# Attention pass A masked through the 32 empty contraction rows, pass B one and a half quads behind it

## The reference

```python
x = x + 0.5 * ffn(layernorm(x))                  # int4 weights with LoRA
x = x + attention(layernorm(x))                  # the one that is changed
x = x + 0.5 * ffn(layernorm(x))
x = x + 0.5 * moe(layernorm(x))
x = x + linear_attention(layernorm(x))
x = x + 0.5 * moe(layernorm(x))

def attention(x, W_attn, W_proj):                # 16 heads of 16
    q, k, v = split(x @ W_attn.T)
    sets = [(i*L, (i+1)*L - 1) for L in (4, 8, 16, ..., 1024) for i in range(T // L)]
    K, V = sums of k, v over each set            # 511 sets
    logits = where(t >= last token of the set, q @ K.T * scale, -inf)
    tail   = sum(q * K_tail) * scale             # the open block of four tokens
    att = softmax(concat(logits, tail))
    out = att[..., :-1] @ V + att[..., -1:] * V_tail
    return out @ W_proj.T
```

## Time and profile before

| | us |
|---|---|
| median of 3 runs | 1737.92 (1735.68 to 1743.44) |
| profiled execution | 1737.69 |
| its span, first to last instruction | 1736.0 |
| TensorE busy | 1433.7 (83%) |
| VectorE busy | 988.1 (57%) |
| ScalarE busy | 689.3 (40%) |
| GpSimd busy | 561.6 (32%) |

### The profile page before, as it was taken

The page is one execution under the profiler, slowest core; times in us unless marked ns, Lnnn a source line. Parts: engine busy times, 40 slices in busy tenths (PEclk is TensorE's granted clock), DMA queues, the critical chain, the costliest instruction groups (busy, mean ns, idle before and its releaser), DMA issues. The chain is left out here.

```text
span 1736.0 us, 26631 instructions
## 1 busy us (share of the span) xinstructions
PE 1433.7 (83%) x9328; PEld 1075.2 (62%) x9328; DVE 988.1 (57%) x2872; ACT 689.3 (40%) x1640; POOL 561.6 (32%) x465
## 2 busy tenths in 40 slices
PE   6899899999999678439999998388994379899894
PEld 5566544555554455228888887365662369788793
DVE  8887777787873597875531111366675945421120
ACT  4222157666667376325423222013334445222221
POOL 6522300000000342304536564322212143447634
PEclk9989989999999898559999999699996579999997
DMA  3034552333300032315869894510114146779963
GB/s 107 19 130 134 136 117 57 81 57 81 57 26 2 1 109 85 149 29 159 250 173 318 241 254 95 137 37 25 49 62 173 22 111 221 201 232 237 278 188 42
DMA packets 113475, 211.82 MB, mean 122 GB/s; under 512 B 20069, under 2 KB 79370, under 8 KB 104138
## 3 DMA queue, kind: packets, MB, share of 16 engines
q1 hardware_dynamic: 87338, 178.93, 32.2%
q0 software_dynamic: 26016, 31.34, 11.6%
HBM read 158.71 MB, written 51.12 MB: 121 GB/s over the span
## 5 line engine op out<-in xcount | busy, mean ns | idle before, releaser
L952 DVE TENSOR_REDUCE attnm_top<-psum 128x1 f32<-128x384 f32 (+3 forms) x384 | 212.7, 596 | 56.5 <-PE psum L1037 52.3
L1174 ACT ACTIVATE attnm_prob<-psum 128x512 f32<-128x512 f32 (+1 forms) x384 | 192.1, 530 | 86.3 <-PE psum L1047 79.7
L2545 DVE SCALAR_TENSOR_TENSOR moe2e_h<-moe2e_gate,psum 128x160 f32<-128x160 f32 x160 | 50.3, 320 | 206.4 <-ACT moe2e_gate L2481 164.3
L2413 PE MATMUL psum<-moe2e_xgT,moe_w_up 128*128 128x160 f32 x1024 | 154.3, 309 | 11.5 <-ACT moe2e_xgT L2490 6.0
L2545 DVE SCALAR_TENSOR_TENSOR moe1e_h<-moe1e_gate,psum 128x160 f32<-128x160 f32 x160 | 50.1, 320 | 193.5 <-ACT moe1e_gate L2481 152.1
L2413 PEld LDWEIGHTS psum<-moe2e_xgT,moe_w_up 128*128 128x128 f32 x1024 | 148.5, 197 | 14.8 <-issue 13.9
L2344 POOL DMA_INDIRECT out<-moe2e_y,moe_scatter_i x74 | 116.5, 1574 | 118.8 <-DMA out<-moe2e_y,moe_scatter_i 54.5
L2344 POOL DMA_INDIRECT x_sum<-moe1e_y,moe_scatter_i x74 | 116.8, 1579 | 116.2 <-DMA x_sum<-moe1e_y,moe_scatter_i 57.3
L2413 PE MATMUL psum<-moe1e_xgT,moe_w_up 128*128 128x160 f32 x1024 | 149.5, 302 | 4.6 <-ACT moe1e_xgT L2490 2.8
L2413 PEld LDWEIGHTS psum<-moe1e_xgT,moe_w_up 128*128 128x128 f32 x1024 | 143.5, 192 | 8.2 <-issue 7.2
L1348 POOL DMA_INDIRECT moe_xg<-xn_rows,moe_gather_i x80 | 83.8, 1048 | 164.6 <-DVE moe_gather_i L1537 93.0
(11 more groups left out here) (420 smaller groups left out, 3110.5 us busy)
## 6 DMA issues: line engine op xcount, KB each, us to landing
moe_w_up<-in_expert_up SPq DMA_DIRECT2D x64, 1024.0 KB
moe_w_down<-in_expert_down SPq DMA_DIRECT2D x64, 512.0 KB
attnm_q_hat<-q_parts SPq DMA_DIRECT2D x72, 128.0 KB, 4.4
moe_a_up<-in_adapter_up SPq DMA_DIRECT2D x32, 256.0 KB
q_parts<-attnf_q_part SPq DMA_DIRECT2D x12, 512.0 KB, 2.8
attnm_k_hat<-k_parts SPq DMA_DIRECT2D x72, 64.0 KB, 2.3
x_res<-in_x SPq DMA_DIRECT2D x8, 512.0 KB
v_tails<-attnf_v_tail SPq DMA_DIRECT2D x4, 1024.0 KB, 5.3
```

The source lines that it names most:

```text
L952: nc.vector.tensor_reduce(top[:, n // QUADS % 2, tiles[0]:tiles[-1] + 1, hh:hh + 1], s.ps[:, u.bank, 0:len(tiles) * width].rearrange("p (t ...
L1174: nc.scalar.activation(prob[:, i % NPROB, at:GROUP], s.ps[:, u.bank, at:GROUP], ACT.Exp).then_inc(taken[u.bank], 1)
L2413: ins = nc.tensor.matmul(s.ps[:, u.bank, half * CAP:(half + 1) * CAP], lhsT, xgT[:, q, c, k * CAP:(k + 1) * CAP], start=(c == 0), stop=(c ...
L2545: nc.vector.scalar_tensor_tensor(out=h[:, HELD[n], i, :], in0=gate[:, i, :], scalar=1.0 if i < INTER // P else SCALE_A, in1=s.ps[:, u.bank ...
```

## The change

1. The sets are laid out in blocks of 64 instead of 128, so that the sets ending within token tile i are block i. `larger` and the mask's maker follow; the mask in `mask_f` takes six selects over both halves, one memset and one select. mask_ts and its copy on VectorE go.
2. Pass A has no mask products. The mask is a product of its own rows: rows 96 to 127 of q_hat and k_hat, until now empty, hold a token's and a set's part. A tile takes one product of the 96 rows over the sets of earlier tiles and one of all 128 rows over its own 64. The columns of a head fall from 3584 to 2300; VectorE takes one reduction per tile, eight per head instead of six, over 2300 instead of 2560 columns.
3. These rows are made by GpSimd in the front stage, once, behind the tails of batch 0 (`make_rows`): two memsets, six selects, a memset, two selects, and two copies that repeat them over k_first (2048 elements per partition) and q_first (4096). SP writes them to HBM; `load_rows` brings them with each quad, 32 rows for quads 1 to 4 (128 and 256 KB), the three that B overwrites for the later ones.
4. B overwrites row 96 to 98 of k_hat with ones and of q_hat with the maxima, so GpSimd writes the ones after each pass A of a quad, before B: sixteen memsets of 3 x 2048 in its order with the tail multiplications.
5. B runs LAG = 38 slots behind A instead of 48; the output steps keep their distance to B; MT stands before slot 5 instead of 6.
6. SP's order: load(1), load(2), maxima(0), load(3), the weights, and on.

The core of the diff:

```diff
+def load_rows(sp, o, many, k_hat, q_hat, landed):
+    sp.dma_start(k_hat[MROW:MROW + many].rearrange("d h t -> d (h t)"), o.k_rows[0:many]).then_inc(landed, 16)
+    sp.dma_start(q_hat[MROW:MROW + many].rearrange("d h t -> d (h t)"), o.q_rows[0:many]).then_inc(landed, 16)
...
+            def make_rows():
+                chain.link(nc.gpsimd.memset(of_set[:], 0.0))
+                for level in range(LEVELS):
+                    n, step, at = 32 >> level, 1 << level, BLOCK - (BLOCK >> level)
+                    v = of_set[:, at:at + n]
+                    chain.link(nc.gpsimd.affine_select(out=v, in_=v, compare_op=ALU.is_ge, fill=MASKED, base=-MROW - step,
+                                                       pattern=[[-step, n]], channel_multiplier=1))
...
+                def repeat(out, of, width):
+                    many = out.shape[1] * out.shape[2] // width
+                    return nc.gpsimd.tensor_copy(
+                        out.rearrange("p h t -> p (h t)").rearrange("p (n t) -> p n t", t=width),
+                        of.rearrange("p (o t) -> p o t", o=1).broadcast_to([P - MROW, many, width]))
+                repeat(o.k_first[MROW:P], of_set[MROW:P, :], BLOCK).then_inc(rows_made, 1)
+                repeat(o.q_first[MROW:P], of_token[MROW:P, :], P).then_inc(rows_made, 1)
...
+                if b == 0:
+                    pool.wait_ge(tails_made, 1)
+                    make_rows()
...
+    def columns(tile, tiles):
+        first = 0 if tile == tiles[0] else BLOCK * (tiles[0] + 1)
+        own = first + BLOCK * tile - tile % 2
+        return first, own, first + BLOCK * (tile + 1) - (tile + 1) % 2
+
+    LAG = NI + NI // 2 + 2
...
-                if n == 6 and 1 <= i <= NQ:
+                if n == 5 and 1 <= i <= NQ:
                     yield ("MT", i - 1, None, None)
...
-                if b:
-                    yield b[n]
+                if 0 <= NI * i + n - LAG < len(second):
+                    yield second[NI * i + n - LAG]
...
-            for n in range(1, RQ - 1):
-                load(n)
-            sp.dma_start(wp[:], wproj_dram.rearrange("(k p) f -> p k f", p=P)).then_inc(wp_in, 16)
-            router.load(sp)
+            load(1)
+            load(2)
             for i in range(1, NQ + 1):
                 maxima(i - 1)
+                if i == 1:
+                    load(3)
+                    sp.dma_start(wp[:], wproj_dram.rearrange("(k p) f -> p k f", p=P)).then_inc(wp_in, 16)
+                    router.load(sp)
...
+            def ones(n):
+                u = u_a[n, QUAD - 1, len(A_TILES) - 1]
+                pool.wait_ge(full[u.bank], u.after(0))
+                nc.gpsimd.memset(k_hat[n % RQ][MROW:MROW + NPART].rearrange("d h t -> d (h t)"), 1.0).then_inc(ones_made, 1)
+                pool.wait_ge(ones_made, n + 1)
...
-                for i, tile in enumerate(A_TILES[t]):
-                    width = (tile // 2 + 1) * P
-                    out = s.ps[:, u.bank, i * width:(i + 1) * width]
-                    nc.tensor.matmul(out[:, width - P:width], s.identb[:], o.mask_ts[:, tile % 2, :], start=(i == 0), stop=False,
-                                     skip_group_check=True)
-                    ins = nc.tensor.matmul(out, q_hat[r][0:MROW, h, tile * P:(tile + 1) * P], k_hat[r][0:MROW, h, 0:width],
-                                           start=False, stop=True, skip_group_check=True)
+                for tile in A_TILES[t]:
+                    first, own, end = columns(tile, A_TILES[t])
+                    rows = slice(tile * P, (tile + 1) * P)
+                    if own > first:
+                        nc.tensor.matmul(s.ps[:, u.bank, first:own], q_hat[r][0:MROW, h, rows], k_hat[r][0:MROW, h, 0:own - first],
+                                         start=True, stop=True, skip_group_check=True)
+                    ins = nc.tensor.matmul(s.ps[:, u.bank, own:end], q_hat[r][:, h, rows], k_hat[r][:, h, own - first:end - first],
+                                           start=True, stop=True, skip_group_check=True)
```

140 lines of the change are left out of this document (82 added, 58 removed).

## The result

The changed kernel is 0.9% slower: 1759.55 us median (1751.75 to 1769.0) against 1740.68 us (1735.68 to 1746.32) for the kernel before in the same comparison, a ratio of 1.0086 with a 95% interval of 1.0053 to 1.0119. The prediction was 1727.3 us, in a range of 1706 to 1748. The profiled execution took 1751.75 us with a span of 1750.0 us, 14.0 us over the span of before.

A forecast was written before the change was run, and what follows sets the result against it. TensorE was taken to lead the attention stages, VectorE and ScalarE close behind. Start -5.3, end and length +1.0, mixed quads -15.1 and front stage +9 sum to -10.4 us from 1737.69: 1727.3 us, range 1706 to 1748.

The forecast's parts named there:

- What bounds the kernel: Attention stages: TensorE sets the pace as a rule, VectorE and ScalarE not far behind; VectorE bounds pass A alone.
- TensorE in pass A, -1.7 us: Pass A products: fewer columns, small products at 0.04 us each, save 0.43 us per head, 1.7 us per quad.
- VectorE -0.5 us: Pass A reductions: eight instead of six per head over 2300 elements take 11.8 us per quad, 0.5 us less.
- Mixed quads, -1.05 us: Quads where passes A and B alternate: each 1.05 us shorter, -15.1 us over 14.4 quads.
- period-by-period reasoning: Mixed quad in three periods of eight slots: 7.2, 5.7 and 5.7 us, 18.6 against 19.65 us.
- 0.3 us per quad, again 1.05: Output quads: 1.35 us gain from TensorE less 0.3 us for MT waiting behind O2 in bank 7, again 1.05 us.
- Costed at nothing: Side work put at no cost: first-stage masks, two more issues per load, sixteen memsets of ones, later tail values.
- the memset of ones holds the maxima: Rival, end of each quad's pass A: maxima wait up to 1.76 us, sixteen times, +28, 1755 us; chance 0.12.
- Start of the stage, -5.3 us: Before pass B begins: fewer A slots first, but transfers land the maxima near 222 us instead of 227.76; bounds -6.5 to -2.
- The bound for load(1): Stage start: load(1) arrives late for A(1), leaving a gain of only 2 us.
- End, -8 us; ten more mixed slots, +9: Shorter lag: ten slots of B alone vanish at the end, -8 us; ten more slots are mixed, +9.0 us.
- The front stage, +9 us: Batch 0: GpSimd's two row copies, 9.4 us, hold VectorE, so TensorE waits; +9 us, 5 to 12, 0 if nothing held.

The follow-up runs named there:

- schedule-only kernel: The kernel before with the change's lag of 38 slots, its banks, moved output steps and MT ahead of slot 5, without the masks: 1737.99 us, 1.0043.
- both causes are mended: The changed kernel with MT ahead of slot 2 and the memset of ones released by MT: 1713.45 us, 0.9945.
- the best kernel: The changed kernel with MT ahead of slot 2, ones released by MT, and mask rows made behind the second batch row's tails: 1708.37 us, 0.9907.

## Why the prediction was wrong, step by step

**What bounds the kernel.** Right for before and, by the time of the quads, for those without output. It missed how a quad with output steps hangs together once TensorE is not full: every hold on VectorE and every wait in bank 7 comes back to TensorE within the quad.

**TensorE in pass A, -1.7 us; VectorE -0.5 us.** Nearly right. Three small products of after start at 318.62, 318.65 and 318.68 us at full clock, 0.03 us apart, the lower bound (0.04 was taken). TensorE's busy time in a quad without output fell from 19.0 to 17.6 us, 1.4 instead of 1.7. From 235 to 530 us the reductions keep VectorE busy for 168.1 us with 428 of them, 0.393 us each with eight a head, where it was 0.559 (182.7 for 327) with six: per quad 12.6 instead of 13.4 us, 0.8 instead of 0.5 less.

**Mixed quads, -1.05 us.** Right in direction, and somewhat small, where nothing else disturbs: in the mean 19.8 to 18.3 us without output (19.0 in the schedule-only kernel, so 0.9 from the schedule and 0.6 from the masks), 23.9 to 22.6 with three output steps once both causes are mended. The mixed stretch of that kernel is 294.6 us, 7.6 under before; the sum had 6.1 less (303.7 to 297.6 in the windows). The period-by-period reasoning behind the number was not tested, so that the sum comes near is no proof of it.

**"0.3 us per quad, again 1.05": the first step that failed.** MT behind O2 was seen, with its wait, and sized from one row (0.97 us, twice before, three times after). It costs 0.8 to 1.0 us in every three-step quad (24.7 to 23.7, 24.0 to 23.1) and about as much in a two-step one (23.0 to 22.2 without the masks), some 0.7 us per quad over a batch of four, where 0.3 was taken. The row gave the wait of one instruction; what was left out is the chain behind it, O3 for MT's copy, VectorE for O3, the next scores for VectorE.

**"Costed at nothing": the second.** The term put at nothing is worth 8.3 us in the changed kernel's mixed stretch (0.8% of the whole). In the kernel before the sixteen memsets added 14.1 us to the mixed stretch and 16.5 us to the whole, and with the masks and the old lag 19.4 and 24 us (1.0104 against 0.9966; the slower of the two also has four dips of the clock in the stage and a wait of 3.19 us instead of 0.53 for the second maxima's rows). The text weighed 1.76 + 0.62 us against 2.6 us of remaining VectorE work "behind the last A". The trace has the maxima 1.3 us (358.91 to 360.21) or 0.7 us (424.26 to 425.00) behind the memset's start: the three reductions thought to be left were one or two. The rival "the memset of ones holds the maxima" had the place, a held VectorE and 1755 us, with a chance of 0.12. But it had the length wrong (0.4 to 1.3 us a quad, not 1.76), it named two instructions that read two tensors (the maxima have three: L963, L967, L970), while what the memset held was the copy with one input, and it was only part of the cause. That 1755 lies near the measured time is luck.

**The clock.** Not in the prediction at all. By the estimate above some 10 us of the 20.7 us that the mixed stretch missed are dips to 1.2 GHz.

**Start of the stage, -5.3 us.** Measured -2.3 to -2.7. B(0) waits 3.35 us for the maxima's rows, A(1) 2.39 us for load(1), both at a DMA share over 1.0 and 156 GB/s, less than the 170 of before that the sum used, and at a clock of 0.50 (before 0.82) in the whole window. The bound for load(1) was in the text; -2 was right. SP's new order was needed for it (8.01 us of waiting in the schedule-only kernel). The second maxima's rows were not costed: before does not wait for them, and seven of the eight kernels with the change's order wait 0.5 to 3.2 us.

**End, -8 us; ten more mixed slots, +9.** Measured -7.6 to -8.3 for the end, and the like times of both lags speak for the pair, with MT's slot as a second difference.

**The front stage, +9 us.** +3.1 of the 4.3 us (the stage before it ends 1.2 us later, within what these runs vary). The copies took 1.89 + 3.60 us, 0.9 ns per element, at the lower bound. The mechanism was right, the place only partly: by the durations, most of what was held beyond before was held by the sums that the rows had pushed back. TensorE's wait of 2.94 us grew to 8.16, not to about 12. The sum was +9, 0 to 12 were its bounds.

**Behind the stage, 0.** Measured 1171.5 us before and 1176.5 after from the last exponential to the end; the four kernels of the next comparison, whose instructions there are the same, have 1163.3 to 1175.0, and those of the two later ones 1151.6 to 1157.6. So +5.0 is within what the same work varies by, and nothing is read from it.

**Sum.** -10.4 forecast; +14.0 profiled = 4.3 - 2.4 + 14.7 - 7.6 + 5.0, in the table's columns. The mixed stretch carries the miss, and what the runs show of it is the two failed steps and the dips of the clock.

## What to carry to other kernels

An instruction given to an idle engine is not free because the engine is idle: look at which instruction of the other engines runs at that moment, and release it by an event behind the delicate chain (here the turn of the maxima), not by the first event that permits it. When a step is moved next to another that uses the same bank, follow the whole chain of releases behind it, not the one wait that the trace shows. And once TensorE has slack, look at its granted clock beside its waits: the dips here followed standstills, though not every one, and were fewer in the kernels with less of them. And when a load is issued ahead of another, look at the waits for the next two as well.

## What the runs showed of the hardware

- A GpSimd memset of 3 x 2048 holds VectorE's instructions with one input in SBUF (tensor_scalar, cast) until it ends: 0.18 us became 0.87. It does not hold one with two inputs in SBUF: L1031 ran at 425.00 us beside the memset in 0.19 us, and in 0.191 to 0.195 us in all sixteen quads of after, in fifteen of which the memset was running. A GpSimd instruction that reads, the tail values' product, holds both kinds (cast 0.49 for 0.18; L983 of before with the memset 0.55 us for 0.19, mean 0.415), but not an instruction with two inputs that started no later than the product (L1035 and L1038 of after at 360.79 and 361.54 us, 0.19 us). The Trainium skill (GPSIMD Engine Reference, Specifications) says that contention is with VectorE instructions in a 2-port mode or with two SBUF inputs; the rows beside the tail values' product fit that. Beside the memset, instructions with one SBUF input were held (no row tells in which mode they ran) and those with two were not, so for the memset the trace shows at most the first half of that rule.
- VectorE holds GpSimd too: in the kernel with the rows made later, a select of 0.2 us at 89.64 us took 2.19, beside a VectorE instruction with two SBUF inputs of 2.29 us that began at 89.48.
- A bfloat16 product of 63 to 65 columns with its own weight load starts every 0.03 us at full clock (318.62, 318.65, 318.68 us) and 0.05 us behind its neighbour at half clock (207.37, 207.42, 207.47 us).
- GpSimd's copy from float32 to bfloat16, 32 partitions, takes 0.9 ns per element (4096 in 3.60 us), less than half of its strided float32 copy of the earlier trace rows (512 in 1.11 us).
- The same quad took 24.4, 25.5 and 27.0 us at a mean clock of 1.00, 0.93 and 0.87.
- Issuing load(2) behind the first maxima took away a wait of 2.83 us for the maxima's rows and made two others, 2.87 us for the third quad and 7.37 instead of 2.97 us for the second maxima. With fewer loads issued the queues moved 107 GB/s at a share of 0.64 up to the first exponential, and 147 at 1.06 in the 16 us behind it; the best kernel has 155 at 1.03 ahead of it. Order did not add bandwidth.
